# The stages of a transformer block in another sequence on every engine

## The chip, the cores and the metric

The kernel runs on one core of a Trainium2 chip. The metric is the device time of one execution in microseconds, the median over runs. PE is TensorE, DVE VectorE, ACT ScalarE, POOL GpSimd and SP SyncE, which issues most transfers.

## The reference

One layer over x of shape (2, 1024, 128): attention with 16 heads of 8 (layer norm of queries and keys per head, rotary turn, causal mask), then a mixture of 16 experts of 64, of which each token takes 2, and a shared one of 128.

```
x = x + attn(layernorm(x))
q, k = rope(headnorm(x @ Wq.T)), rope(headnorm(x @ Wk.T)); v = x @ Wv.T
out = softmax(mask(q k^T / sqrt(8))) v @ Wo.T + bo
x = x + ffn(layernorm(x))
s = softmax(x @ gate_w.T); groups of 4: keep 2 of 4 groups, then the 2 largest
y = sum_e combine[t, e] * ((silu(x We1 + be1) * (x We3 + be3)) We2 + be2)
z = silu(x ws1 + bs1) * (x ws3 + bs3) @ ws2 + bs2; return x + y + z
```

## The kernel before

The 2048 tokens are cut into four chunks of 512 (x = 0 to 3). Chunks 0 and 1 are the first halves of the two sequences, 2 and 3 the second halves. Heads go in four groups per chunk, so there are 16 attention blocks (a = 0 to 15). Each stage has a name with its indices, such as `scores.14.0`. All of them stand once in one long word list, `ORDER` (from line 132). Every engine walks the same list (`for kind, arg in SCHEDULE`) and issues the stages that are its own, so the list sets each engine's order, and semaphores set the rest. Behind an @ stand the PSUM banks that a PE stage fills; a fill waits until the reader of the bank's last fill is done (`wait_read`, line 592 on). Banks 0 to 5 are used in pairs by maxima and scores, bank 6 holds single fills and the sum of the experts, bank 7 the attention sum. Each engine executes its queue in order: a waiting stage holds what is behind it.

The stages by engine:
- PE: `xT`, `qkv` (line 635), `qT`, `kT` and other turns (626), `max` (644, 672: products whose maxima are wanted), `mturn` (681), `scores` (695, with the mask 644), `pv` (718), `proj` (728), `gate` (736), `moeU`, `moeV`, `moeG`, `moeL` (766), `moe_y` (782, 786), `wide` (758). Maxima and scores load 62 or 64 rows, two at a time in the array; `pv` loads 18 columns, four at a time; the products of 128 by 128 take the whole array.
- DVE: `norm`, `norm2` (1111 to 1127: for norm2.3 a chain of eleven small operations, each waiting for the one before), `headsum`, `maxred` (1159), `oturn`, `oT_read` (1174, 1176), `oback`, `proj_read`, `route1` to `route3` (1213 to 1242: the router's small chains), `moe_a` (1249), `moe_m` (1257), `moe_h_dve`, `final`.
- ACT: `exp` (842), the reads of `qkv` (858 to 862), `qT_lead`, `kT_lead`, `qT_mid`, `kT_mid` (bf16 parts of queries and keys), `norm_apply`, `norm2_apply` (923), `mcopy`, `moe_v`, `moe_t`, `moe_s`, and for chunk 0 the transfers of the keys' parts (`stack_act`).
- POOL: `norm_rstd`, `norm2_rstd` (1011 to 1020), `rstd_pool` (995 to 1002), `rope_pool` (472 to 478), `rope_join` (486, 487), `tables_pool` (449 to 454), `mneg` (1033, 1034: negated maxima split in two), `qT_low`, `kT_low` (1041), `moe_one` (1077), `moe_g` (1084), `moe_h` (496), `xbo`.
- SP: input transfers first, then `stack` (parts into q_st and k_st, line 507), `mrow` (567), `cstore`, `cload`, `store`.

The exponentials use eight slots, the values of the experts four (`V_RING`) and their products nine (`T_RING`), so `moe_v` waits for `moe_g` of three units earlier and `moe_t` for `moe_y` of nine earlier. A chunk's rotary chain is headsum, rstd_pool, rope_pool, rope_join, then qT and kT, the three parts and their transfers, then the maxima of the chunk.

Of the kernel before, what the change touches and what calls it, by code (L numbers as in the profile page):

```python
# [132 lines left out]
weights.0@5 ones.0 norm.0 weights_read.0 xT.0@6 xT_read.0 qkv.0@3 norm.1 norm_rstd.1 qkv_read.0 qkv.1@2 qkv_read.1  # L133
qkv.2@3 qkv.3@4 qkv_read.2 qkv_read.3 tables.0 norm_apply.1 xT.1@3 norm.2 xT_read.1 qkv.4@1 qkv.5@6 headsum.0 headrstd.0
rope.0 ones.1 qkv_read.4 qkv_read.5 qkv.6@5 qkv_read.6 qkv.7@0 qkv_read.7 qT.0@4 kT.0@3 norm_rstd.2 norm_apply.2
qT_lead.0 stack.0.0.0 kT_lead.0 qT_rest.0 qT_mid.0 xT.2@5 xT_read.2 kT_rest.0 kT_mid.0 halved.0 qkv.8@2 tables_pool.0
stack_act.0.1.0 headsum.1 qkv.9@4 qkv.10@0 qkv.11@6 qT_low.0 norm.3 stack_act.0.1.1 kT_low.0 stack_act.0.1.2 stack.0.0.2
qkv_read.8 qkv_read.9 qkv_read.10 qkv_read.11 stack.0.0.1 max.0.0@45 maxred.0.0 max.0.1@23 maxred.0.1 max.0.2@45
maxred.0.2 max.0.3@01 max.0.4@23 maxred.0.3 maxred.0.4 max.0.5@01 max.1.0@23 maxred.0.5 maxred.1.0 max.1.1@45 maxred.1.1
max.1.2@01 rstd_pool.1 rope_pool.1 maxred.1.2 max.1.3@23 maxred.1.3 max.1.4@45 maxred.1.4 mneg.0 mturn.0@0 mcopy.0  # L140
max.1.5@01 max.2.0@23 max.2.1@45 maxred.1.5 maxred.2.0 maxred.2.1 max.2.2@23 mrow.0 scores.0.0@01 exp.0.0 weights2.0@6
maxred.2.2 scores.0.1@45 max.2.3@01 maxred.2.3 max.2.4@23 maxred.2.4 weights2_read.0 exp.0.1 rope_join.1 qT.1@6 kT.1@5
scores.1.0@01 max.2.5@23 qT_lead.1 qT_rest.1 stack.1.0.0 kT_lead.1 exp.1.0 mneg.1 mturn.1@4 mcopy.1 qT_mid.1 kT_rest.1
mrow.1 pv.0 max.3.0@45 norm_rstd.3 norm_apply.3 maxred.2.5 mneg.2 maxred.3.0 kT_mid.1 scores.1.1@01 max.3.1@23
maxred.3.1 max.3.2@45 xT.3@6 exp.1.1 headsum.2 stack.1.1.0 scores.2.0@23 scores.3.0@01 maxred.3.2 qT_low.1 kT_low.1
stack.1.1.2 stack.1.0.1 xT_read.3 qkv.12@6 exp.2.0 exp.3.0 max.3.3@23 max.3.4@45 maxred.3.3 maxred.3.4 qkv.13@1 qkv.14@0
max.3.5@23 qkv_read.12 qkv_read.13 qkv_read.14 maxred.3.5 qkv.15@5 stack.1.1.1 stack.1.0.2 qkv_read.15 max.4.0@01
rstd_pool.2 mturn.2@6 mneg.3 max.4.1@23 scores.3.1@45 exp.3.1 rope_pool.2 maxred.4.0 max.4.2@01 pv.1 maxred.4.1
max.4.3@45 maxred.4.2 maxred.4.3 mcopy.2 scores.4.0@23 exp.4.0 max.4.4@01 pv.2 scores.4.1@45 maxred.4.4 max.4.5@23
mturn.3@6 maxred.4.5 mneg.4 scores.5.0@01 exp.4.1 exp.5.0 max.5.0@45 mrow.2 maxred.5.0 scores.6.0@23 mcopy.3 headsum.3  # L150
scores.6.1@01 max.5.1@45 pv.3 exp.6.0 mturn.4@6 exp.6.1 max.5.2@23 mcopy.4 rope_join.2 scores.7.0@01 exp.7.0 maxred.5.1
maxred.5.2 max.5.3@45 maxred.5.3 pv.4 pv.5 oturn.0 scores.7.1@23 max.5.4@45 maxred.5.4 scores.8.0@01 exp.7.1 xbo.0
qT.2@6 mrow.3 exp.8.0 scores.9.0@23 oT_read.0 max.5.5@45 maxred.5.5 qT_lead.2 qT_rest.2 scores.9.1@01 pv.6 exp.9.0
# [1240 lines left out]
```

## Time and profile before

| what | us |
|---|---|
| median of 3 runs | 383.33 |
| lowest and highest | 382.54, 387.38 |
| the profiled execution | 383.55 |
| its span, first to last instruction | 381.7 |
| granted clock of TensorE, mean | 0.95 |

The span leaves out what lies around the first and the last instruction, 1.85 us here. A matmul's duration in the rows holds its way through the array, so consecutive ones overlap, and the distance of their starts tells more than their length. A name such as `mx_diag` or `probs` is a tile; "<-" points from what is read to what is written. In the table by stage the five busy columns are PE, PEld (weight loads), DVE, ACT, POOL.

### The profile page before, as it was taken

The numbers are of one execution on the slowest core, as the hardware profiler recorded it, in microseconds if no ns is written. First come the engines' busy times: TensorE is split into PE (matmuls) and PEld (weight loads), VectorE is DVE, ScalarE is ACT, GpSimd is POOL, SyncE is SP. The second block draws the span as 40 slices with busy tenths as digits, with TensorE's granted clock in tenths as the row PEclk, the third lists the DMA queues.
The fourth block names the chain that finished last, engine by engine and source line by source line (L and its number), as shares of the span: only waits on it lengthen the run. The fifth ranks groups of instructions, "written<-read, shape, count | busy, mean of one in ns | idle before, by whom it ended". The sixth has DMA issues, their size and how long they took to land.

```text
span 381.7 us, 7937 instructions
## 1 busy us (share of the span) xinstructions
PE 338.2 (89%) x2883; PEld 148.3 (39%) x2883; DVE 291.7 (76%) x508; ACT 233.5 (61%) x340; POOL 181.1 (47%) x304
## 2 busy tenths in 40 slices
PE   2667689899799898999999989999999999969995
PEld 1233345445444334353334332434334433434342
DVE  5693789899999999779998899987686830656742
ACT  1656129776759566774576767786676999424320
POOL 1587985998855438657504502034060028471000
PEclk9966559999999999999999999999999999988999
DMA  4997004103200036002043130001000019000000
GB/s 124 200 217 162 16 3 127 43 3 92 78 3 4 0 106 149 2 0 72 0 100 87 38 75 2 3 1 30 2 2 2 3 53 202 0 0 0 3 27 27
DMA packets 26840, 19.65 MB, mean 51 GB/s; under 512 B 9713, under 2 KB 23570, under 8 KB 26738
## 3 DMA queue, kind: packets, MB, share of 16 engines
q1 hardware_dynamic: 25410, 18.09, 20.8%
q10 hardware_dynamic: 1392, 1.05, 1.2%
q8 instruction: 24, 0.39, 0.5%
q14 instruction: 14, 0.11, 0.1%
HBM read 11.56 MB, written 1.15 MB: 33 GB/s over the span
## 4 chain that ended last, share of the span: by engine, by line
PE 61%; DVE 24%; issue 5%; ACT 5%; DMA 2%; POOL 1%; ACTq 1%; SPq 1%; DVEq 0%; POOLq 0%
PE psum L766 14%; PE psum L718 13%; PE psum L782 7%; PE psum L695 7%; PE psum L672 7%; DVE mx_diag L1159 7%; PE psum L644 5%; DVE mx_full L1159 4%; ACT probs L842 2%; PE psum L626 2%; DVE mv L1249 2%; PE psum L635 1%; PE psum L736 1%; PE psum L728 1%; DVE resid L1148 1%
## 5 line engine op out<-in xcount | busy, mean ns | idle before, releaser
L842 ACT ACTIVATE probs<-psum 128x1024 f32<-128x1024 f32 x144 | 142.3, 1024 | 49.7 <-PE psum L644 27.1
L1159 DVE TENSOR_REDUCE mx_diag<-psum 128x4 f32<-128x512 f32 (+2 forms) x96 | 96.0, 1041 | 23.3 <-PE psum L672 22.6
L1159 DVE TENSOR_REDUCE mx_full<-psum 128x2 f32<-128x1024 f32 x64 | 76.1, 1220 | 7.3 <-PE psum L672 7.0
L718 PE MATMUL psum<-probs,v_ones 128*18 128x512 f32 (+3 forms) x768 | 73.6, 489 | 0.2
L766 PE MATMUL psum<-x2T,w 128*128 128x512 f32 x144 | 71.8, 626 | 1.0 <-DVE mv L1249 0.9
L672 PE MATMUL psum<-k_st,q_st 62*128 62x512 bf16 (+3 forms) x384 | 60.6, 344 | 2.0 <-ACT probs L842 0.9
L644 PE MATMUL psum<-masks 64*128 64x128 bf16 (+2 forms) x896 | 51.5, 216 | 11.0 <-DVE mx_diag L1159 3.3
L695 PE MATMUL psum<-q_st,k_st 64*128 64x512 bf16 (+3 forms) x384 | 53.7, 328 | 3.1 <-DVE mv L1249 0.9
L644 PEld LDWEIGHTS psum<-masks 64*128 64x128 bf16 x896 | 33.6, 96 | 42.8 <-DVE mx_diag L1159 14.9
L1077 POOL TENSOR_SCALAR mh<-mh 128x512 f32<-128x512 f32 x27 | 16.8, 623 | 62.3 <-ACT mh L895 62.1
L1084 POOL TENSOR_TENSOR mh<-mh,mv 128x512 f32<-128x512 f32 x27 | 34.1, 1270 | 11.8 <-DVE mv L1249 11.8
L766 PEld LDWEIGHTS psum<-x2T,w 128*128 128x128 f32 x144 | 25.7, 195 | 29.5 <-issue 24.4
L782 PE MATMUL psum<-mh,w 128*128 128x512 f32 x72 | 37.1, 624 | 0.0
L496 POOL TENSOR_TENSOR mh<-mh,early 128x512 f32<-128x512 f32 x24 | 30.6, 1287 | 12.6 <-DMA early<-combine_scratch 12.4
L695 PEld LDWEIGHTS psum<-q_st,k_st 64*128 64x128 bf16 x384 | 17.4, 94 | 41.8 <-ACT probs L842 18.1
L672 PEld LDWEIGHTS psum<-k_st,q_st 62*128 62x128 bf16 x384 | 20.2, 100 | 22.3 <-ACT probs L842 9.7
L1249 DVE SCALAR_TENSOR_TENSOR mv<-psum,b,mv 128x512 f32<-128x512 f32 x27 | 19.6, 743 | 9.7 <-ACT mh L895 9.3
L718 PEld LDWEIGHTS psum<-probs,v_ones 128*18 128x18 f32 x768 | 16.7, 97 | 25.3 <-issue 22.8
L886 ACT ACTIVATE mv<-psum,b3h 128x512 f32<-128x512 f32 x27 | 18.4, 687 | 11.0 <-PE psum L766 10.6
L1033 POOL CAST negmax<-mx_diag 128x16 bf16<-128x16 f32 x16 | 3.2, 198 | 43.3 <-DVE mx_diag L1324 40.2
L895 ACT ACTIVATE mh<-psum,b1h 128x512 f32<-128x512 f32 x27 | 18.5, 688 | 6.5 <-PE psum L766 6.4
L635 PE MATMUL psum<-w_qkv,xnT 128*128 128x384 f32 x32 | 19.0, 750 | 2.8 <-ACT xnT L848 2.7
(162 smaller groups left out, 359.0 us busy)
## 6 DMA issues: line engine op xcount, KB each, us to landing
early<-combine_scratch SPq DMA_DIRECT2D x24, 256.0 KB, 4.8
q_st<-parts SPq DMA_DIRECT2D x24, 128.0 KB, 2.4
k_st<-parts SPq DMA_DIRECT2D x18, 128.0 KB, 2.4
w<-in_We SPq DMA_DIRECT2D x3, 512.0 KB
k_st<-in_c_pad SPq DMA_DIRECT2D x8, 128.0 KB, 6.3
out<-xs SPq DMA_DIRECT2D x4, 256.0 KB, 2.3
xs<-in_x SPq DMA_DIRECT2D x3, 256.0 KB, 5.9
k_st<-parts ACTq DMA_DIRECT2D x6, 128.0 KB, 4.0
```

The source lines that it names most:

```text
L496: engine.tensor_tensor(h, h, comb_b[:, u, :], ALU.mult).then_inc(weighted, 1)
L635: pe.matmul(w[:, 0:3 * P], xnT[:, t * P:(t + 1) * P], w_qkv[:, :], start=True, stop=True).then_inc(work_full, 1)
L644: return pe.matmul(dst, masks[r, slot, :], blocked, start=start, stop=stop, skip_group_check=True)
L672: last = pe.matmul(w[:, par, i * keys:(i + 1) * keys], q_st[r, x % 2, 2 * g + m, q0:q0 + P], k_st[r, b, 2 * g + m, k0:k0 + keys], start=(w ...
L695: last = pe.matmul(w[:, par, col:col + cols], k_st[rows(par), b, 2 * g + m, kt * P:(kt + 1) * P], q_st[rows(par), x % 2, 2 * g + m, q0:q0 ...
L718: last = pe.matmul(acc[32 * j:32 * j + 2 * VC, q0:q0 + cols], own_then_zeros, probs[:, n % P_RING, j % 2, col:col + cols], start=(kt == 0 ...
L766: pe.matmul(w, (w1 if kind in ("moeU", "moeG") else w3)[:, unit(n), :], x2T[:, x % 2, :], start=True, stop=True).then_inc(work_full, 1)
L782: last = pe.matmul(y, w2[:, unit(n), :], mh[:, at % T_RING, :], start=(n == 0), stop=(n == UNITS - 1), skip_group_check=True)
L842: act.activation(probs[:, n % P_RING, :, :], wpair("scores", (s, i)), ACT.Exp, scale=SCALE).then_inc(exp_done, 1)
L1084: pool.tensor_tensor(t, t, mv[:, at % V_RING, :], ALU.mult).then_inc(gate_done, 1)
L1159: dve.tensor_reduce(dst[:, a % 2, :, pairs[0]:pairs[0] + nm, qt], w, AX.X, ALU.max, negate=True).then_inc(max_free, 1)
L1249: dve.scalar_tensor_tensor(out=v, in0=wbank("moeU", (x, n)), scalar=b1[:, unit(n):unit(n) + 1], in1=v, op0=ALU.add, op1=ALU.mult).then_inc ...
```

## The change

Only `ORDER` changes: the same 1316 words, each once, in another sequence, and other banks behind many PE stages. No function changes. Since every engine walks the list, this alters the order on PE, DVE, ACT, POOL and SP at once. The diff, cut to the stretches that the next sections speak of:

```diff
--- before.py
+++ after.py
@@ -130,127 +130,126 @@
 
 
 ORDER = """
-weights.0@5 ones.0 norm.0 weights_read.0 xT.0@6 xT_read.0 qkv.0@3 norm.1 norm_rstd.1 qkv_read.0 qkv.1@2 qkv_read.1
-qkv.2@3 qkv.3@4 qkv_read.2 qkv_read.3 tables.0 norm_apply.1 xT.1@3 norm.2 xT_read.1 qkv.4@1 qkv.5@6 headsum.0 headrstd.0
-rope.0 ones.1 qkv_read.4 qkv_read.5 qkv.6@5 qkv_read.6 qkv.7@0 qkv_read.7 qT.0@4 kT.0@3 norm_rstd.2 norm_apply.2
-qT_lead.0 stack.0.0.0 kT_lead.0 qT_rest.0 qT_mid.0 xT.2@5 xT_read.2 kT_rest.0 kT_mid.0 halved.0 qkv.8@2 tables_pool.0
-stack_act.0.1.0 headsum.1 qkv.9@4 qkv.10@0 qkv.11@6 qT_low.0 norm.3 stack_act.0.1.1 kT_low.0 stack_act.0.1.2 stack.0.0.2
-qkv_read.8 qkv_read.9 qkv_read.10 qkv_read.11 stack.0.0.1 max.0.0@45 maxred.0.0 max.0.1@23 maxred.0.1 max.0.2@45
-maxred.0.2 max.0.3@01 max.0.4@23 maxred.0.3 maxred.0.4 max.0.5@01 max.1.0@23 maxred.0.5 maxred.1.0 max.1.1@45 maxred.1.1
-max.1.2@01 rstd_pool.1 rope_pool.1 maxred.1.2 max.1.3@23 maxred.1.3 max.1.4@45 maxred.1.4 mneg.0 mturn.0@0 mcopy.0
-max.1.5@01 max.2.0@23 max.2.1@45 maxred.1.5 maxred.2.0 maxred.2.1 max.2.2@23 mrow.0 scores.0.0@01 exp.0.0 weights2.0@6
-maxred.2.2 scores.0.1@45 max.2.3@01 maxred.2.3 max.2.4@23 maxred.2.4 weights2_read.0 exp.0.1 rope_join.1 qT.1@6 kT.1@5
...
-mrow.1 pv.0 max.3.0@45 norm_rstd.3 norm_apply.3 maxred.2.5 mneg.2 maxred.3.0 kT_mid.1 scores.1.1@01 max.3.1@23
...
-exp.9.1 max.6.0@45 max.6.1@23 maxred.6.0 scores.10.0@01 kT.2@6 exp.10.0 maxred.6.1 mrow.4 scores.10.1@45 max.6.2@23
-maxred.6.2 max.6.3@01 kT_lead.2 exp.10.1 pv.7 rstd_pool.3 max.6.4@45 scores.11.0@23 exp.11.0 maxred.6.3 maxred.6.4
-max.6.5@01 stack.2.1.0 maxred.6.5 stack.2.0.0 pv.8 mneg.5 pv.9 max.7.0@45 qT_mid.2 kT_rest.2 kT_mid.2 stack.2.1.1
-max.7.1@23 scores.12.0@01 exp.12.0 pv.10 pv.11 maxred.7.0 maxred.7.1 mturn.5@4 mcopy.5 oturn.1 oT_read.1 oback.0
-scores.12.1@01 exp.12.1 scores.13.0@45 exp.13.0 max.7.2@23 maxred.7.2 rope_pool.3 scores.13.1@01 proj.0@6 proj_read.0
-norm2.0 exp.13.1 scores.14.0@23 exp.14.0 mrow.5 scores.15.0@01 max.7.3@45 pv.12 scores.15.1@23 exp.15.0 exp.15.1
-maxred.7.3 stack.2.0.1 max.7.4@01 qT_low.2 kT_low.2 mneg.6 mturn.6@6 max.7.5@45 scores.16.0@23 maxred.7.4 exp.16.0
-stack.2.0.2 stack.2.1.2 max.8.0@01 mcopy.6 maxred.7.5 maxred.8.0 norm2_rstd.0 norm2_apply.0 max.8.1@23 max.8.2@45 mneg.7
-maxred.8.1 pv.13 pv.14 pv.15 mturn.7@1 maxred.8.2 max.8.3@23 x2T.0@6 maxred.8.3 max.8.4@45 mcopy.7 x2T_read.0 maxred.8.4
-scores.16.1@01 max.8.5@23 exp.16.1 maxred.8.5 gate.0@6 gate_read.0 max.8.6@01 moeV.0.0@5 moeV.0.1@3 moe_v.0.0 maxred.8.6
...
-exp.73.1 scores.74.0@45 pv.70 route1.2 route2.2 exp.74.0 route3.2 cT.2@0 pv.71 cT_read.2 moe_t.2.2 moe_one.2.2
-scores.74.1@23 moe_a.2.2 moe_g.2.2 exp.74.1 moeV.2.4@4 moeU.2.3@0 cstore.2 moe_t.2.3 moe_one.2.3 moe_v.2.4 moe_a.2.3
-moe_g.2.3 moeV.2.5@1 moe_v.2.5 moeU.2.4@6 moe_t.2.4 scores.75.0@45 moe_one.2.4 scores.75.1@23 scores.76.0@01 moe_a.2.4
-store.1 cload.2.0 moe_h.2.1 pv.72 pv.73 pv.74 exp.75.0 exp.75.1 exp.76.0 scores.76.1@45 exp.76.1 scores.77.0@23 pv.75
-scores.77.1@45 moe_g.2.4 scores.78.0@01 exp.77.0 exp.77.1 moeU.2.5@6 exp.78.0 scores.78.1@45 scores.79.0@23 exp.78.1
-exp.79.0 pv.76 pv.77 pv.78 pv.79 cload.2.2 oturn.7 moeV.2.6@3 cload.2.1 moeV.2.7@1 moeV.2.8@4 moe_t.2.5 moe_a.2.5
-moe_h.2.2 moe_v.2.6 moe_v.2.7 moeU.2.6@2 moeU.2.7@0 moeU.2.8@1 oT_read.7 oback.3 proj.3@5 moe_v.2.8 moe_t.2.6 moe_t.2.7
-moe_h.2.3 moe_h.2.4 moe_one.2.5 moe_one.2.6 moe_a.2.6 moe_y.2.0 moe_one.2.7 moe_t.2.8 moe_one.2.8 cload.2.3 moe_y.2.1
-moe_y.2.2 moe_y.2.3 proj_read.3 norm2.3 norm2_apply.3 x2T.3@5 x2T_read.3 moe_g.2.5 moe_g.2.6 moe_h.2.5 moe_a.2.7
-moe_y.2.4 moe_g.2.7 moe_a.2.8 moe_g.2.8 gate.3@3 gate_read.3 moeG.3.0@5 moeG.3.1@0 moe_h.2.6 gate_exp.3 moe_s.3.0
-moe_s.3.1 route1.3 route2.3 moeG.3.2@3 moeG.3.3@1 moeL.3.0@5 moeL.3.1@4 moe_m.3.0 moe_m.3.1 moeL.3.2@2 moe_s.3.2
-moe_h.2.7 moe_s.3.3 moe_y.2.5 moe_h.2.8 route3.3 moe_y.2.6 moe_y.2.7 moe_y.2.8 y_leave.2 moeG.3.4@1 moe_s.3.4 moeG.3.5@4
-moe_s.3.5 moe_m.3.2 moeL.3.3@5 comb3.3 cT3.3@2 moe_m.3.3 moeL.3.4@6 moeL.3.5@0 cT3_read.3 wide.3.1@1 moe_m.3.4 moe_m.3.5
-moe_h_dve.3.1 wide.3.2@4 moe_h_dve.3.2 wide.3.3@2 wide.3.4@6 wide.3.5@3 moeG.3.6@5 moe_h_dve.3.3 moe_h_dve.3.4
-moeG.3.7@1 moe_h_dve.3.5 moe_s.3.6 moe_s.3.7 moeL.3.6@4 moe_m.3.6 moeL.3.7@0 yturn.2@3 moe_y.3.0 final.2 store.2 cT.3@4
-wide.3.6@1 moe_m.3.7 wide.3.7@5 wide.3.8@2 cT_read.3 moe_y.3.1 moe_y.3.2 moeG.3.8@0 moe_h_dve.3.6 moe_h_dve.3.7
-moe_y.3.3 moeL.3.8@4 moe_s.3.8 moe_m.3.8 moe_y.3.4 moe_y.3.5 moe_h_dve.3.8 moe_y.3.6 moe_y.3.7 moe_y.3.8 y_leave.3
-yturn.3@2 final.3 store.3
+ones.0 ones.1 weights.0@5 weights_read.0 norm.0 tables.0 xT.0@3 xT_read.0 qkv.0@1 qkv.1@0 norm.1 qkv_read.0 qkv_read.1
+qkv.2@6 qkv_read.2 qkv.3@1 qkv_read.3 norm_rstd.1 norm_apply.1 xT.1@5 xT_read.1 qkv.4@0 qkv.5@6 qkv_read.4 qkv_read.5
+qkv.6@2 qkv_read.6 qkv.7@5 norm.2 qkv_read.7 headsum.0 headrstd.0 rope.0 qT.0@1 qT_lead.0 stack.0.0.0 norm_rstd.2 kT.0@0
+kT_lead.0 headsum.1 qT_rest.0 kT_rest.0 stack_act.0.1.0 qT_mid.0 kT_mid.0 qT_low.0 stack_act.0.1.1 norm_apply.2 kT_low.0
+xT.2@2 stack_act.0.1.2 weights2.0@4 xT_read.2 weights2_read.0 stack.0.0.1 stack.0.0.2 max.0.0@45 max.0.1@23 maxred.0.0
+maxred.0.1 max.0.2@01 maxred.0.2 max.0.3@45 maxred.0.3 qkv.8@6 max.0.4@01 qkv_read.8 maxred.0.4 max.0.5@45 maxred.0.5
+max.1.0@23 maxred.1.0 max.1.1@01 qkv.9@6 rstd_pool.1 rope_pool.1 maxred.1.1 max.1.2@23 max.1.3@01 maxred.1.2 maxred.1.3
+mneg.0 max.1.4@45 qkv.10@2 qkv_read.9 qkv_read.10 maxred.1.4 rope_join.1 max.1.5@01 mturn.0@5 maxred.1.5 max.2.0@23
+maxred.2.0 max.2.1@01 mcopy.0 maxred.2.1 qkv.11@4 qkv_read.11 max.2.2@23 maxred.2.2 qT.1@4 norm.3 qT_lead.1 qT_rest.1
+kT.1@0 kT_lead.1 kT_rest.1 mrow.0 scores.0.0@23 exp.0.0 max.2.3@45 maxred.2.3 mneg.1 mturn.1@6 scores.0.1@23 norm_rstd.3
+qT_mid.1 max.2.4@01 stack.1.0.0 max.2.5@45 exp.0.1 maxred.2.4 scores.1.0@23 scores.1.1@01 kT_mid.1 mcopy.1 mrow.1
+stack.1.1.0 exp.1.0 pv.0 maxred.2.5 scores.2.0@23 exp.1.1 exp.2.0 norm_apply.3 headsum.2 max.3.0@01 max.3.1@45 qT_low.1
...
+max.4.2@45 maxred.4.0 maxred.4.1 max.4.3@01 mrow.2 maxred.4.2 qkv.13@6 qkv_read.13 max.4.4@23 max.4.5@45 rstd_pool.2
+mneg.3 pv.3 maxred.4.3 pv.4 mturn.3@6 tables_pool.0 mcopy.3 maxred.4.4 maxred.4.5 max.5.0@23 rope_pool.2 maxred.5.0
+scores.5.0@01 max.5.1@45 maxred.5.1 scores.6.0@23 mrow.3 exp.5.0 exp.6.0 pv.5 halved.0 oturn.0 mneg.4 scores.6.1@45
...
+exp.9.1 mneg.5 scores.10.0@45 scores.10.1@01 max.6.2@23 maxred.6.2 exp.10.0 exp.10.1 rstd_pool.3 qT.2@6 qT_lead.2
+max.6.3@45 max.6.4@23 maxred.6.3 scores.11.0@01 exp.11.0 pv.8 pv.9 xbo.0 mturn.5@5 qT_rest.2 mcopy.5 mrow.4 max.6.5@01
+maxred.6.4 maxred.6.5 max.7.0@45 maxred.7.0 kT.2@6 mrow.5 kT_lead.2 stack.2.1.0 kT_rest.2 scores.12.0@23 exp.12.0
+max.7.1@01 stack.2.0.0 maxred.7.1 scores.12.1@45 exp.12.1 pv.10 pv.11 scores.13.0@45 qT_mid.2 kT_mid.2 oturn.1
+scores.13.1@23 pv.12 exp.13.0 oT_read.1 oback.0 max.7.2@01 maxred.7.2 stack.2.0.1 scores.14.0@45 exp.13.1 exp.14.0
+mneg.6 proj.0@6 scores.15.0@23 exp.15.0 qT_low.2 proj_read.0 kT_low.2 norm2.0 scores.15.1@45 exp.15.1 pv.13 max.7.3@23
+maxred.7.3 scores.16.0@01 norm2_rstd.0 exp.16.0 max.7.4@45 mturn.6@2 mcopy.6 max.7.5@01 maxred.7.4 maxred.7.5
+rope_pool.3 stack.2.1.1 scores.16.1@23 exp.16.1 stack.2.1.2 stack.2.0.2 max.8.0@45 pv.14 maxred.8.0 pv.15 mneg.7
+max.8.1@23 max.8.2@01 norm2_apply.0 scores.17.0@45 exp.17.0 maxred.8.1 maxred.8.2 pv.16 max.8.3@23 mrow.6 x2T.0@6
+x2T_read.0 max.8.4@01 maxred.8.3 scores.18.0@45 maxred.8.4 max.8.5@23 maxred.8.5 gate.0@6 gate_read.0 moeV.0.0@1
+exp.18.0 gate_exp.0 moe_v.0.0 max.8.6@45 maxred.8.6 scores.18.1@23 exp.18.1 route1.0 moeV.0.1@6 moe_v.0.1 mturn.7@0
+mcopy.7 moeU.0.0@1 route2.0 max.8.7@45 max.8.8@23 moeV.0.2@0 moe_v.0.2 moe_t.0.0 moeU.0.1@6 moe_t.0.1 maxred.8.7
+maxred.8.8 rope_join.3 moe_a.0.0 moe_a.0.1 moeV.0.3@0 pv.17 moe_v.0.3 max.8.9@45 scores.19.0@01 exp.19.0 scores.19.1@23
+maxred.8.9 moeU.0.2@6 exp.19.1 scores.20.0@45 mrow.7 scores.21.0@01 max.8.10@23 exp.20.0 oturn.2 pv.18 scores.21.1@45
+exp.21.0 exp.21.1 route3.0 maxred.8.10 moe_one.0.0 moe_t.0.2 moe_g.0.0 pv.19 moe_one.0.1 pv.20 cT.0@5 cT_read.0
+max.8.11@01 scores.22.0@23 exp.22.0 maxred.8.11 max.8.12@45 max.8.13@01 maxred.8.12 maxred.8.13 mmin.8 mneg.8 xbo.1
+moe_a.0.2 qT.3@2 qT_lead.3 qT_rest.3 moeU.0.3@3 moe_t.0.3 moe_a.0.3 kT.3@4 moeU.0.4@5 kT_lead.3 moe_t.0.4 kT_rest.3
...
+exp.74.1 scores.75.0@23 exp.75.0 pv.72 pv.73 scores.75.1@45 scores.76.0@01 yturn.1@2 exp.75.1 exp.76.0 oT_read.6 final.1
+moeV.2.6@6 scores.76.1@45 exp.76.1 cload.2.3 moe_g.2.3 scores.77.0@23 exp.77.0 scores.77.1@01 pv.74 pv.75 exp.77.1
+cload.2.0 moe_h.2.1 moe_h.2.2 scores.78.0@45 exp.78.0 scores.78.1@23 scores.79.0@01 pv.76 pv.77 exp.78.1 pv.78 exp.79.0
+pv.79 moe_v.2.6 oturn.7 moeV.2.7@1 cload.2.1 moeU.2.5@2 moeU.2.6@5 moe_t.2.5 moe_t.2.6 moe_g.2.4 moe_h.2.3 moe_y.2.0
+moeV.2.8@3 moe_v.2.7 moe_v.2.8 oT_read.7 moe_h.2.4 cload.2.2 oback.3 proj.3@4 moeU.2.7@1 moe_a.2.5 moe_t.2.7 moe_a.2.6
+moeU.2.8@2 moe_one.2.5 moe_g.2.5 moe_one.2.6 moe_t.2.8 moe_y.2.1 moe_y.2.2 proj_read.3 norm2.3 norm2_apply.3 x2T.3@4
+moe_one.2.7 moe_a.2.7 x2T_read.3 moe_y.2.3 moeG.3.0@3 moe_a.2.8 moe_g.2.6 moe_h.2.5 moe_h.2.6 moe_g.2.7 moeG.3.1@1
+gate.3@5 moe_h.2.7 gate_read.3 gate_exp.3 route1.3 moe_s.3.0 moe_y.2.4 moe_y.2.5 moe_y.2.6 moeL.3.0@0 moeL.3.1@2
+moeG.3.2@3 moe_y.2.7 moe_s.3.1 moe_m.3.0 moe_m.3.1 moe_one.2.8 moeG.3.3@0 moe_g.2.8 moe_h.2.8 route2.3 route3.3 comb3.3
+moeL.3.2@4 moe_s.3.2 moe_s.3.3 moeL.3.3@5 moeL.3.4@0 moe_m.3.2 moe_m.3.3 moeL.3.5@1 store.1 moe_y.2.8 y_leave.2
+moeG.3.4@2 moeG.3.5@3 moeG.3.6@5 moe_s.3.4 moe_s.3.5 moe_s.3.6 cT3.3@2 cT3_read.3 moeG.3.7@4 moe_s.3.7 moe_m.3.4
+moe_m.3.5 moeL.3.6@3 moe_m.3.6 wide.3.1@0 wide.3.2@1 moe_h_dve.3.1 wide.3.3@5 wide.3.4@2 moe_h_dve.3.2 cT.3@4
+moe_h_dve.3.3 cT_read.3 moe_h_dve.3.4 moe_y.3.0 moe_y.3.1 moeG.3.8@3 yturn.2@1 moe_s.3.8 final.2 wide.3.5@2 wide.3.6@4
+wide.3.7@0 wide.3.8@3 moe_h_dve.3.5 moe_y.3.2 moe_h_dve.3.6 moeL.3.7@5 moeL.3.8@1 moe_y.3.3 moe_m.3.7 moe_h_dve.3.7
+moe_m.3.8 moe_y.3.4 moe_y.3.5 moe_y.3.6 moe_y.3.7 moe_h_dve.3.8 moe_y.3.8 y_leave.3 yturn.3@5 final.3 store.2 store.3
 """
 TOLD = [told(word) for word in ORDER.split()]
 SCHEDULE = [stage for stage, _ in TOLD]

```

## Rows read from the trace of the kernel before

**Rows 1.** The page: busy us, share of the span, instructions of each engine.

```profile
PE 338.2 (89%) x2883; PEld 148.3 (39%) x2883; DVE 291.7 (76%) x508; ACT 233.5 (61%) x340; POOL 181.1 (47%) x304
```

**Rows 2.** Table by stage: stretch, length, engine busy (instructions), clock, DMA share, GB/s.

```profile
40.00:57.00 17.00, 13.64 (x130) 7.26 (x131) 14.83 (x16) 2.47 (x4) 15.21 (x26) 0.50 0.01 1
...
40.80:104.70 63.90, 55.17 (x759) 29.48 (x755) 58.27 (x70) 38.69 (x61) 54.10 (x96) 0.87 0.19 52
...
104.00:325.00 221.00, 211.97 (x1934) 85.34 (x1935) 180.10 (x273) 158.35 (x202) 90.48 (x134) 1.00 0.17 40
...
325.00:382.00 57.00, 49.33 (x140) 21.80 (x132) 30.39 (x82) 16.41 (x26) 12.10 (x12) 0.93 0.03 10
```

**Rows 3.** Waits: who waited for whom, us in total, times, longest.

```profile
ACT probs L842 <- PE psum L644: 27.1, 28, 4.5
```

**Rows 4.** Order of time, 25 to 41 us: start, us, engine, line, operation.

```profile
25.75 0.32 POOL L449 TENSOR_TENSOR g_cos<-rope,gb 128x64 f32<-128x64 f32 x1
...
30.05 0.46 POOL L454 TENSOR_TENSOR g_add<-g_add,mh 128x128 f32<-128x128 f32 x1
...
30.65 4.50 SPq L507 DMA_DIRECT2D q_st<-parts  x6
...
32.64 3.46 ACTq L507 DMA_DIRECT2D k_st<-parts  x5
...
33.22 0.86 DVE L1111 BATCH_NORM_STATS2 stats<-xs 128x6 f32<-128x128 f32 x4
34.11 0.38 DVE L1114 BATCH_NORM_AGGREGATE mean_var<-stats 128x2 f32<-128x6 f32 x4
...
40.05 0.50 PE L644 MATMUL psum<-masks 64*128 64x256 bf16 x4 [2.75 <-ACT v_ones L862]
```

**Rows 5.** Order of time, PE at 172 us: three whole-array pairs, then a 64-row pair.

```profile
172.12 1.12 PE L782 MATMUL psum<-mh,w 128*128 128x512 f32 x2
173.09 1.02 PE L766 MATMUL psum<-x2T,w 128*128 128x512 f32 x2
173.94 1.02 PE L782 MATMUL psum<-mh,w 128*128 128x512 f32 x2
174.90 0.39 PE L672 MATMUL psum<-k_st,q_st 62*128 62x512 bf16 x2
```

**Rows 6.** Order of time, POOL, 91 to 111 us: rope_pool.3, norm2_rstd.0, mneg.7, rope_join.3.

```profile
91.59 2.37 POOL L472 TENSOR_TENSOR early<-early,hrstd 128x1024 f32<-128x1024 f32 x1
...
101.47 0.20 POOL L1011 TENSOR_SCALAR nr_pool<-mean_var 128x4 f32<-128x4 f32 x1 [0.44 <-DVE mean_var L1114]
...
106.39 0.22 POOL L1034 TENSOR_TENSOR negmax<-mx_diag,negmax 128x16 bf16<-128x16 f32 x1
...
108.61 2.35 POOL L487 TENSOR_TENSOR roped<-roped,early 128x1024 f32<-128x1024 f32 x1
```

**Rows 7.** Order of time: line 1233 beside a POOL product, and with POOL idle.

```profile
120.54 1.23 DVE L1233 TENSOR_TENSOR beats<-beats 128x64 f32<-128x64 f32 x1
...
120.40 1.28 POOL L1084 TENSOR_TENSOR mh<-mh,mv 128x512 f32<-128x512 f32 x1
...
346.62 0.22 DVE L1233 TENSOR_TENSOR beats<-beats 128x64 f32<-128x64 f32 x1
```

**Rows 8.** Order of time: the chain of norm2.3 on DVE, and POOL beside it.

```profile
334.68 1.19 DVE L1099 TENSOR_SCALAR seed<-rstd 128x4 int32<-128x4 int32 x1
335.91 0.16 DVE L1101 SCALAR_TENSOR_TENSOR nr<-seed 128x4 f32<-128x4 f32 x1
...
334.58 1.26 POOL L496 TENSOR_TENSOR mh<-mh,early 128x512 f32<-128x512 f32 x1
```

**Rows 9.** Order of time, PE, 325 to 340 us: the tail's start.

```profile
325.32 5.42 PE L766 MATMUL psum<-x2T,w 128*128 128x512 f32 x12
330.58 1.05 PE L728 MATMUL psum<-w_o,o_normT 128*128 128x128 f32 x8
...
339.57 0.66 PE L626 MATMUL psum<-ident,w_raw 128*128 128x128 f32 x4 [3.26 <-ACT w_raw L923]
```

More of the change, by code:

```diff
@@ L148 @@
[L148 to L152, printed above, removed]
@@ new lines @@
+moe_h.0.1 moe_h.0.2 moe_a.0.6 qT_mid.3 proj_read.1 norm2.1 moeU.0.7@0 exp.26.0 moe_one.0.5 moeU.0.8@6 scores.26.1@23
+moe_t.0.7 moe_a.0.7 cload.0.2 moe_one.0.6 exp.26.1 max.9.8@45 maxred.9.8 pv.24 norm2_rstd.1 scores.27.0@23 max.9.9@01
+moe_t.0.8 scores.27.1@45 pv.25 exp.27.0 scores.28.0@23 exp.27.1 maxred.9.9 moe_a.0.8 exp.28.0 max.9.10@01 max.9.11@45
+maxred.9.10 moe_y.0.0 maxred.9.11 max.9.12@01 maxred.9.12 max.9.13@23 maxred.9.13 max.10.0@45 moe_y.0.1 norm2_apply.1
+kT_mid.3 x2T.1@2 x2T_read.1 moe_y.0.2 maxred.10.0 scores.28.1@01 exp.28.1 max.10.1@23 maxred.10.1 scores.29.0@45
@@ new lines @@
+moe_g.0.5 exp.29.0 moe_g.0.6 moe_h.0.3 moe_h.0.4 moe_y.0.3 moe_one.0.7 moe_one.0.8 max.10.2@01 max.10.3@23 maxred.10.2
+maxred.10.3 moe_g.0.7 moe_g.0.8 moe_h.0.5 moe_h.0.6 max.10.4@45 moe_y.0.4 maxred.10.4 moeV.1.0@0 moe_v.1.0 gate.1@1
+moeV.1.1@2 gate_read.1 moeV.1.2@0 gate_exp.1 route1.1 moe_v.1.1 moe_v.1.2 max.10.5@45 mmin.9 mneg.9 scores.29.1@23
+maxred.10.5 exp.29.1 moeU.1.0@1 moeU.1.1@0 moe_t.1.0 moe_a.1.0 moe_t.1.1 moe_a.1.1 moeU.1.2@3 moe_t.1.2 moe_a.1.2
+moeV.1.3@2 moe_v.1.3 moe_y.0.5 max.10.6@45 maxred.10.6 max.10.7@23 maxred.10.7 mturn.9@1 mcopy.9 moeU.1.3@0 moe_t.1.3
@@ new lines @@
+scores.56.1@23 exp.56.1 cload.1.3 maxred.14.3 max.14.4@01 maxred.14.4 pv.54 max.14.5@45 max.14.6@23 mneg.13 mturn.13@1
+mcopy.13 pv.55 max.14.7@01 maxred.14.5 maxred.14.6 scores.57.0@45 exp.57.0 moeU.1.8@6 max.14.8@23 max.14.9@45
+maxred.14.7 norm2_rstd.2 maxred.14.8 norm2_apply.2 scores.57.1@01 moe_h.1.2 moe_g.1.6 mrow.13 exp.57.1 max.14.10@23
+maxred.14.9 moe_t.1.8 moe_g.1.7 maxred.14.10 moe_a.1.8 pv.56 scores.58.0@45 exp.58.0 scores.59.0@01 exp.59.0 yturn.0@2
+final.0 x2T.2@6 x2T_read.2 max.14.11@45 max.14.12@23 maxred.14.11 maxred.14.12 scores.59.1@01 exp.59.1 pv.57 pv.58
@@ new lines @@
+scores.68.0@45 scores.68.1@23 oturn.6 exp.67.1 exp.68.0 exp.68.1 moe_g.1.8 moe_y.1.6 moe_y.1.7 moe_g.2.0 moe_h.1.8
+moe_y.1.8 y_leave.1 moe_g.2.1 scores.69.0@23 scores.69.1@45 scores.70.0@01 pv.66 pv.67 exp.69.0 exp.69.1 exp.70.0
+scores.70.1@23 exp.70.1 pv.68 mmin.15 mneg.15 mturn.15@5 mcopy.15 scores.71.0@01 scores.71.1@23 scores.72.0@45 exp.71.0
+exp.71.1 exp.72.0 route1.2 route2.2 route3.2 moeV.2.3@6 moe_v.2.3 moeU.2.3@1 moeV.2.4@3 moeV.2.5@0 moeU.2.4@6 moe_t.2.3
+mrow.15 moe_g.2.2 moe_v.2.4 moe_v.2.5 cT.2@2 cT_read.2 cstore.2 pv.69 moe_a.2.3 scores.73.0@23 scores.73.1@01
```

130 lines of the change are left out of this document (53 added, 77 removed).

## The prediction

> **What bounds the kernel now.** I read the page's busy times first: TensorE (PE) is busy for 338.2 of 381.7 us, VectorE (DVE) for 291.7, ScalarE for 233.5, GpSimd (POOL) for 181.1 [rows 1]. The table by stage [rows 2] says where this matters. From 104 to 325 us PE is busy 212.0 of 221.0 us and DVE 180.1: there PE sets the pace and idle DVE time is free. From 40.8 to 104.7 us DVE is busy 58.3 of 63.9 and POOL 54.1, PE 55.2: three engines are nearly full. From 40 to 57 us the granted clock is 0.50, so PE is at 1.2 GHz. The first 40 us wait for input: the first maxima start at 40.05 us, right after the last of the 12 transfers of split queries and keys that were issued from 30.65 us on [rows 4]. The tail after 325 us is one dependent chain with PE work laid into its gaps. The waits [rows 3] show that the longest wait of ScalarE, 27.1 us, ends on PE's products, which agrees with PE as the pace.
>
> **The change part by part.** Every stage is in both lists, once, so instruction counts and sizes are equal and only positions and PSUM banks differ. I sum for each engine, from the durations in the trace, what stands ahead of a stage in the old and in the new list; a PE stage counts with its start-to-start time where nothing waits (whole-array product 0.85 to 0.86 us, qkv 0.65 at full clock, pv 0.86 for two banks, maxima and scores 0.22 to 0.39).
>
> *PE's tile shapes.* With three shapes (64 rows for maxima and scores, 18 columns for probabilities times values, the whole array for the rest; the small turns counted with their column width) the old list changes shape 236 times, the new one 244 times, so the runs don't get longer as a whole. The price: a whole-array pair starts 0.85 us before the next one of its shape, and 0.96 us before a 64-row one [rows 5], 0.11 us. 8 x 0.11 = +0.9 us. By stretch the counts are 46 and 54 between max.0.0 and max.8.0, 181 and 181 from there to the last pv, 8 and 8 in the tail: all eight more lie in the first, and its sum below holds them. The Trainium skill, TensorEngine Tiling (Array Packing), section Key Properties, says that changing the tiling mode drains the engine. By that rule the new list would pay for more drains and not fewer; the trace agrees on the sign, and its 0.11 us is used.
>
> *Up to 40 us.* The four qkv products of chunk 2, norm.3, halved and tables_pool leave the shadow of the input transfers; ScalarE issues the transfers of the leading keys before its two middle parts and before norm_apply.2. The first of these can't leave before 28.9 us, and 12 transfers of 128 KB share the queues, so max.0.0 starts at about 39.7 us instead of 40.05: -0.3 us, between -0.8 and +0.5. weights2 now stands ahead of it and asks for 11 input transfers, which were issued before the ones that the maxima wait for, so it costs nothing.
>
> *40 to 104 us.* DVE takes norm.3 (0.86 + 0.38 us [rows 4]) and halved (0.3) here, +1.6 us; it has 5.6 us idle in this stretch [rows 2], so between 0 and 1.6 of it shows, and I take 1.0 because the idle pieces are short and the maxima queue behind each reduction. PE takes the four qkv products (2.6 us), and pv.13 (0.9) and scores.16.1 (0.4) come ahead of max.8.0, weights2 (0.3) leaves, and there are the eight changes of shape: +4.5 us at full clock from max.0.0 to max.8.0, of which 1.3 are taken from the next stretch. It has 8.7 us idle here and pays half clock for the first 17 us, where four products are 5.1 us against 2.6 us. Covered if DVE stays the slower one; if not, up to +2.5. POOL takes tables_pool, from 25.75 to 30.5 us before [rows 4], 4.8 us, between mneg.3 and rope_pool.2: it was free and now stands in a full stretch. rope_join.2 ends 4.8 us later, at about 87.5 us; behind it on POOL wait mneg.5, rstd_pool.3, mneg.6 and the low parts of chunk 2. The reader of rope_join.2 is the turn qT.2, which has 44.2 us of PE work ahead of it instead of 38.7, 5.5 us more, so the delay is covered by 0.7 us.
>
> *The second POOL shift.* rope_pool.3 (6.7 us) stood before norm2_rstd.0 and fills 91.6 to 98.2 us; now it follows it. norm2_rstd.0 waits for DVE's statistics at 101.5 us in either order [rows 6], a little over 1 us later now, so POOL idles before it, ends it at 107.4, rope_pool.3 at 114.1, mneg.7 at 114.6 (106.6 before), rope_join.3 at 119.0 (111.0 before). mneg.7 releases mturn.7, which has 67.0 us of PE work ahead of it, 58.8 before; PE reached that sum at 116.2 us. Slack 1.6 us, cost 0. x2T.0 needs norm2_apply.0 at 109.2 us and PE reaches it near 110.6.
>
> *104 to 325 us.* PE's sum from max.8.0 to pv.79 is 1.4 us smaller: pv.13, scores.16.1 and moeU.2.5 are gone from it, moeV.2.6 came in, and nothing changes in the count of shapes: -1.4 us. On DVE, short operations that read two SBUF operands last until a running POOL instruction ends: 1.23 us against 0.22 free, beside a POOL product of 1.28 us [rows 7]. route2 and route3 of chunks 0 and 1 and two o_norm scalings lose 6.9 us in all to this. In the new list route2.1, route3.0, route3.1 and these scalings have POOL waiting or busy with little; route1.0 and route2.0 fall beside rope_join.3, whose two instructions can hold them for up to 3 us. Net DVE gain 3.9 us. As PE is 96% busy in this stretch I let a third pass, -1.2 us; bounds 0 and -3.9.
>
> *The tail.* Between the last pv and proj.3 stand six products, 325.32 to 330.58 us [rows 9]; now five, and proj.3's input is ready at 328.3 us in either order: -0.9 us. Against it stands norm2.3, the chain of eleven tiny operations on which all that follows waits. Two of them were held by POOL (1.19 us for one of 0.16 [rows 8]), then POOL ran out of work. In the new order moe_one.2.7, moe_g.2.6, moe_h.2.5 and moe_h.2.6 lie beside the chain, so three or four are held: +1.2 us, between 0 and +3.6. From x2T.3 to the last product PE's sum grows by 0.8 us: +0.8. The half-clock stretch there begins after PE idles 3.3 us before x2T.3 [rows 9]; the gap stays, so I keep its cost. Tail: -0.9 + 1.2 + 0.8 = +1.1 us.
>
> The Trainium skill, SBUF — State Buffer, section Who interferes with whom, says that a VectorE instruction with two SBUF inputs contends with a GpSimd instruction that reads SBUF and that the loser blocks fully. If every one of the eleven operations met a fresh POOL instruction this would be some 11 us instead of 4; POOL runs out of ready work after four.
>
> Sum: -0.3 + 1.0 + 0 - 1.4 - 1.2 + 1.1 = -0.8 us. The profiled execution took 383.55 us (span 381.7), the median of the runs is 383.33. 383.3 - 0.8 = 382.5 us.
>
> **The rivals.**
> A, the sum holds, the order is worth about nothing (0.58): 382.5 us, own range 378 to 387.
> B, POOL becomes the bound (0.20). For it: 54.1 of 63.9 us busy before, plus 4.8, plus the idle before norm2_rstd.0. Slacks of 0.7 and 1.6 us are thin. Against it: PE work was laid in front of both readers. If mneg.7 comes 9.4 us late instead of 8 and the queries of chunk 2 miss their place, maxima of chunk 2 (max.8.0) start late and each turn waits; it decides from a slip of some 3 us, and gives 383.3 + 4.8 to + 9.4, so about 390.
> C, DVE is the hidden pace (0.20). For it: in 40.8 to 104.7 us DVE is fullest. If all contention goes (6.9 us), and PE's idle 9.0 us from 104 to 325 halves, it gives 383.3 - 1.4 - 6.9 = 375 us. Against it: PE is 96% busy when the contention occurs.
> D, norm2.3 is held at nearly every step (0.02 alone, part of the upper range): 11 x 1.1 = 12 us minus the 2.1 already paid, 392 us. Against: POOL's four instructions are 4.4 us long.
>
> **How the numbers follow.** A is likeliest, so 382.5 us. The range reaches into B and C: 376 to 391. Over 2% faster means under 375.7, slower means over 391.0, about what a measurement of this kernel can tell from no change. C lies on the first limit and gives 0.16 with a little of A; B and D give 0.19; within 2% is 0.65.
>
> **What would show it.** max.0.0 at 39 to 40.5 us. max.8.0 at 104.5 to 106 us, with POOL busy through 57 to 99 us. mneg.7 near 114.6 us and no wait of mturn.7 for it over 1 us; a wait there is B. Routing stages of chunk 1 free of held operations, and route1.0 or route2.0 held. The last pv at 323 to 326 us: earlier than 320 is C. norm2.3 taking 5.5 to 8 us, and proj.3 4.3 us after the last pv. I am wrong if PE's small waits, 8.7 us idle from 40.8 to 104.7 and 9.0 from 104 to 325 [rows 2], change by more than 4 us, because no row prices them one by one.

## The result, and the profile after

The new kernel takes 389.81 us in the median, the kernel before 383.28 us beside it: ratio 1.0191, 95% interval 1.0161 to 1.022, so 6 to 8 us slower. The first profiled execution of the new kernel was a disturbed one of 1067 us; all rows of the new kernel below are from a second profiled execution of the same kernel, which took 391.47 us (span 389.6).

The page of the new kernel, busy times (they answer to [rows 1]) and the granted clock in 40 slices:

```profile
PE 337.5 (87%) x2883; PEld 145.8 (37%) x2883; DVE 294.9 (76%) x508; ACT 234.5 (60%) x340; POOL 178.0 (46%) x304
...
PEclk9965899999998999999899998999999999978999
```

The same row of the kernel before:

```profile
PEclk9966559999999999999999999999999999988999
```

The busy times hardly moved, but the row of the clock has single digits of 8 in the middle, where the kernel before has 9 throughout. The table by stage (columns as in [rows 2]) and three short stretches around those digits:

```profile
40.00:57.00 17.00, 12.44 (x122) 6.42 (x117) 16.76 (x26) 6.47 (x17) 14.09 (x20) 0.93 0.02 5
40.80:104.70 63.90, 54.98 (x779) 28.92 (x775) 59.13 (x80) 43.48 (x73) 50.96 (x101) 0.99 0.19 52
104.00:325.00 221.00, 208.50 (x1806) 81.43 (x1803) 181.17 (x273) 151.29 (x193) 89.95 (x133) 0.98 0.14 33
...
124.00:128.00 4.00, 4.00 (x32) 1.59 (x34) 3.66 (x13) 2.95 (x4) 0.97 (x2) 0.57 0.01 2
185.00:189.00 4.00, 4.00 (x40) 1.38 (x40) 3.47 (x7) 0.71 (x1) 0.00 (x0) 0.59 0.02 6
233.00:237.00 4.00, 4.00 (x26) 0.87 (x24) 3.29 (x4) 1.84 (x3) 0.25 (x2) 0.57 0.00 0
```

Three times between 104 and 325 us TensorE falls to its lower level (1.2 GHz) for most of 4 us; in [rows 2] it ran at 1.00 in this whole stretch. And PE idles 221.0 - 208.5 = 12.5 us there against 9.0 before; time at half clock counts as busy in this column. The first 17 us of maxima run nearly at full clock now (0.93 against 0.50), which brings little, because DVE is busy for 16.76 of 17.

Where the time went, from the starts of the same stages in both traces (us from start to start):

| stretch | before | new | difference |
|---|---|---|---|
| start to max.0.0 | 40.05 | 39.04 | -1.0 |
| max.0.0 to max.8.0 | 63.74 | 65.86 | +2.1 |
| max.8.0 to pv.79, the last pv | 220.99 | 227.07 | +6.1 |
| pv.79 to proj.3 | 5.80 | 4.94 | -0.9 |
| proj.3 to x2T.3 | 9.00 | 10.34 | +1.3 |
| x2T.3 to final.3 | 38.73 | 38.95 | +0.2 |

The sum is +7.9 us, and the stretch that was to get 2.6 us shorter got 6.1 us longer. PE waits in three places there. The first, in order of time (columns as in [rows 7]):

```profile
115.39 2.39 DVE L1215 TENSOR_TENSOR lg<-lg,gate_bb 128x64 f32<-128x64 f32 x1
...
115.35 2.35 POOL L486 TENSOR_TENSOR roped<-roped,early 128x1024 f32<-128x1024 f32 x1
...
121.85 0.34 PE L643 MATMUL psum<-masks 64*128 64x256 bf16 x4 [1.78 <-DVE mx_full L1158]
```

One of route1.0's small operations is held for the whole of rope_join.3's second product; route1.0 takes 3.96 us (1.68 free). Behind it on DVE stand route2.0 and the two reductions for whose banks PE waits 1.8 us. The second place:

```profile
178.91 1.30 POOL L1051 TENSOR_TENSOR xs<-xs,bo_b 128x512 f32<-128x512 f32 x1
179.01 1.29 DVE L1230 TENSOR_TENSOR beats<-gsm 128x64 f32<-128x64 f32 x1
...
180.18 2.49 POOL L495 TENSOR_TENSOR mh<-mh,early 128x512 f32<-128x512 f32 x2
180.34 1.20 DVE L1231 TENSOR_TENSOR beats<-beats,lower 128x64 f32<-128x64 f32 x1
...
181.56 1.19 DVE L1232 TENSOR_TENSOR beats<-beats 128x64 f32<-128x64 f32 x1
...
182.79 0.22 DVE L1233 TENSOR_REDUCE gsm<-beats 128x16 f32<-128x64 f32 x1
...
184.84 0.34 PE L643 MATMUL psum<-masks 64*128 64x256 bf16 x4 [2.83 <-DVE mv L1248]
```

POOL has work back to back (xbo.2, moe_h.0.7, moe_h.0.8), and each small operation of route2.1 lasts until one of these ends: 5.03 us for the stage, 1.60 free. moe_a.1.4, whose bank max.10.9 needs, stands behind it. The third place is on the transfers:

```profile
221.86 3.91 SPq L581 DMA_DIRECT2D early<-combine_scratch  x6
226.34 1.41 SPq L566 DMA_DIRECT2D q_st<-maxT  x2
...
231.68 0.39 PE L694 MATMUL psum<-q_st,k_st 64*128 64x512 bf16 x2 [1.51 <-DMA q_st<-maxT]
```

mturn.11 stands 11 us later than before, only 5.9 us ahead of scores.45.0, and SP issues its two small transfers (mrow.11) right behind six of 256 KB with the weights of the experts. After each of the three waits comes one of the three stretches of half clock.

### The profile page after: what moved, and what is told of

The parts are those of the page before. It is cut to its first block, busy times and chain, and to the rows that moved or that the text cites. A ratio compares the mean times of both kernels' runs of the same rounds, so it can differ in the third digit from the quotient of the medians.

```text
span 1065.1 us, 7936 instructions
## 1 busy us (share of the span) xinstructions
PE 1042.4 (98%) x2883; PEld 305.0 (29%) x2883; DVE 295.1 (28%) x508; ACT 241.6 (23%) x340; POOL 175.5 (16%) x304
## 3 DMA queue, kind: packets, MB, share of 16 engines
HBM read 11.56 MB, written 1.15 MB: 12 GB/s over the span
## 4 chain that ended last, share of the span: by engine, by line
PE 97%; ACT 1%; DVE 1%; DMA 0%; ACTq 0%; issue 0%
PE psum L765 23%; PE psum L717 22%; PE psum L781 11%; PE psum L694 11%; PE psum L671 11%; PE psum L643 7%; PE psum L634 4%; PE psum L625 3%; PE psum L785 1%; PE psum L727 1%; PE psum L735 1%; PE psum L743 1%; PE psum L757 1%; DMA xs<-in_x 0%; ACTq L506 0%; ACT early L922 0%
## 5 line engine op out<-in xcount | busy, mean ns | idle before, releaser
L765 PE MATMUL psum<-x2T,w 128*128 128x512 f32 x144 | 246.3, 1926 | 0.0
L717 PE MATMUL psum<-probs,v_ones 128*18 128x512 f32 (+3 forms) x768 | 240.9, 1415 | 0.0
L671 PE MATMUL psum<-k_st,q_st 62*128 62x512 bf16 (+3 forms) x384 | 152.2, 843 | 0.0
L694 PE MATMUL psum<-q_st,k_st 64*128 64x512 bf16 (+3 forms) x384 | 143.5, 833 | 0.2 <-ACT probs L841 0.2
L781 PE MATMUL psum<-mh,w 128*128 128x512 f32 x72 | 124.3, 1915 | 0.0
L643 PE MATMUL psum<-masks 64*128 64x128 bf16 (+2 forms) x896 | 116.5, 418 | 0.7 <-ACT w_o L847 0.4
L643 PEld LDWEIGHTS psum<-masks 64*128 64x128 bf16 x896 | 75.8, 185 | 120.2 <-issue 115.7
L765 PEld LDWEIGHTS psum<-x2T,w 128*128 128x128 f32 x144 | 59.4, 432 | 120.8 <-issue 113.4
L781 PEld LDWEIGHTS psum<-mh,w 128*128 128x128 f32 x72 | 29.4, 428 | 62.4 <-issue 60.6
L634 PE MATMUL psum<-w_qkv,xnT 128*128 128x384 f32 x32 | 41.0, 1443 | 1.5 <-ACT xnT L847 1.5
```

The source lines that it names most:

```text
L634: pe.matmul(w[:, 0:3 * P], xnT[:, t * P:(t + 1) * P], w_qkv[:, :], start=True, stop=True).then_inc(work_full, 1)
L643: return pe.matmul(dst, masks[r, slot, :], blocked, start=start, stop=stop, skip_group_check=True)
L671: last = pe.matmul(w[:, par, i * keys:(i + 1) * keys], q_st[r, x % 2, 2 * g + m, q0:q0 + P], k_st[r, b, 2 * g + m, k0:k0 + keys], start=(w ...
L694: last = pe.matmul(w[:, par, col:col + cols], k_st[rows(par), b, 2 * g + m, kt * P:(kt + 1) * P], q_st[rows(par), x % 2, 2 * g + m, q0:q0 ...
L717: last = pe.matmul(acc[32 * j:32 * j + 2 * VC, q0:q0 + cols], own_then_zeros, probs[:, n % P_RING, j % 2, col:col + cols], start=(kt == 0 ...
L765: pe.matmul(w, (w1 if kind in ("moeU", "moeG") else w3)[:, unit(n), :], x2T[:, x % 2, :], start=True, stop=True).then_inc(work_full, 1)
```

## The experiments

All edits are moves of words in `ORDER`; a word marked - goes, one marked + comes. The new kernel again, unaltered (391.26 us median of two runs, 391.05 and 391.47):

> The changed kernel unaltered, for a profile that can be read against the one before. If POOL became the bound (rival B): mneg.7 near 116 us or later and max.8.0 at 107 us or later, with most of the 6.5 us lost by 110 us. If the loss is in the tail (the chain norm2.3 held by POOL at more steps than four): the last pv before 326 us and norm2.3 longer than 8 us. If it is PE's small waits in between: PE's idle from 104 us to the last pv grows by 4 us or more.

One edit in the new kernel for each of the three places, and all three together (e4):

```diff
 exp.18.1
-route1.0
...
-route2.0
...
 maxred.8.8
+route1.0
+route2.0
```

(e1),

```diff
 scores.29.1@23
+route2.1
 maxred.10.5
...
 cload.0.3
-route2.1
```

(e2), and, as e3,

```diff
 mmin.11
+mneg.11
...
 max.12.3@01
+mturn.11@6
+mcopy.11
+mrow.11
 moeV.1.6@6
...
-mneg.11
...
-mturn.11@5
-mcopy.11
...
-mrow.11
 scores.45.0@01
```

> The new kernel with one edit: route1.0 and route2.0 stand behind maxred.8.7 and maxred.8.8 on DVE instead of ahead of them, so they no longer run inside rope_join.3 while two reductions that PE needs are queued behind them. Held-chain theory (H): the 1.9 us wait of PE before max.8.9 at 121.8 us and the dip of the granted clock at 124.0 to 127.4 us go; worth 1.9 + 1.7 = 3.6 us at most, and I expect 1.5 to 3 us less than the new kernel, about 388 us. Rival (S, the loss is spread over many small waits and does not hang on this place): within 0.7 us of the new kernel, since the wait comes back a few stages later.

Measured: 388.98 us, ratio to the kernel before 1.0179 (1.0099 to 1.0258), 0.8 us less than the new kernel where 1.5 to 3 were expected. There is no dip at 124 us, but the wait moved: 2.2 us before scores.19.0, for moe_a.0.0, which now stands behind both router stages and ends at 122.71 us, 0.15 us ahead of scores.19.0. That the dip is gone can't be laid to the edit: e2 and e3 below leave this place alone and have none there either.

> The new kernel with one edit: route2.1 moves up on DVE from behind moe_a.1.3 (178.9 us, amid six POOL stages back to back) to between mmin.9 and maxred.10.5 (171.4 us, where POOL idles). H: route2.1 takes 1.6 to 2.3 us instead of 5.03, the 2.8 us wait of PE before max.10.9 at 184.8 us and the dip of the granted clock at 185.5 to 188.9 us go; 2.5 to 4.5 us less than the new kernel, about 387 us. S: within 0.7 us of the new kernel.

Measured: 387.0 us, 1.0133 (1.0067 to 1.0199). route2.1 takes 1.59 us, the wait and the dip at 185 us are gone, and the stretch from max.9.0 to max.11.0 fell from 59.1 to 56.1 us. This one is firm: the five profiles with route2.1 in its old place (new, e1, e3, e9, e11) have 58.1 to 60.7 us there, the six with it early (e2, e4, e5, e6, e7, e10) 55.8 to 56.1.

> The new kernel with one edit: mneg.11, mturn.11, mcopy.11 and mrow.11 move up, from 225.8 us to about 216.5 us on PE, ahead of the combine weights' transfers cload.1.x on SP, to bank 6. H: the row of maxima arrives long before scores.45.0, the 1.5 us wait of PE at 231.7 us and the dip of the granted clock at 233.3 to 236.7 us go; 1.5 to 3 us less than the new kernel, about 388.5 us. S: within 0.7 us of the new kernel.

Measured: 387.5 us, 1.0157 (1.0055 to 1.0259). No wait before scores.45.0 and no dip; from max.11.0 to max.15.0 77.2 us instead of 79.4.

> The new kernel with the three edits of the three single runs together. H: the sum of the three, 6 to 9 us less than the new kernel, so 381 to 384 us, equal to the kernel before; no half-clock dip between 110 and 340 us, and the last pv starts at about 325 us. S: less than 2.5 us gained, 387 us or more.

Measured: 384.8 us, 1.0063 (1.0018 to 1.0109), so 5 us less than the new kernel, where 6 to 9 were expected. There is no half clock between 110 and 340 us, and the last pv starts at 325.66 us. The three places are most of the loss. The single runs are not told apart from the new kernel by their times (the intervals overlap), only by their traces; this one is.

Then the router of chunk 0 in other places, and the two theories of the third place. Against e4:

```diff
 maxred.8.8
-route1.0
-route2.0
...
 moe_a.0.1
+route1.0
...
 maxred.8.9
+route2.0
```

(e5, which keeps the edits of e2 and e3), and, as e6, the same without the edit of e3 but with

```diff
 cstore.1
-cload.1.2
-cload.1.1
...
-cload.1.0
...
 mrow.11
+cload.1.2
+cload.1.1
+cload.1.0
 scores.45.0@01
```

> The new kernel with route2.1 and mturn.11 moved as in the run of all three, but with the router of chunk 0 in other places: moe_a.0.0 and moe_a.0.1 first, then route1.0, then maxred.8.9, then route2.0. In the run of all three the wait of PE at 121 us did not go, it moved: 2.2 us before scores.19.0, until moe_a.0.1 had read its bank, which stood behind both router stages. H: with nothing that PE waits for behind two router stages this wait shrinks to under 1 us, and the kernel is 1 to 2.5 us shorter than with all three (384.8), so about 383 us. S: the wait comes back elsewhere, within 0.7 us of 384.8.

Measured: 385.23 us, 1.0063 (1.003 to 1.0096), against what the held-chain theory expected: the wait came back as 1.5 us before scores.20.0 and 1.1 us before pv.18. Both later places for the router only shifted it. (In e4 too the wait before scores.19.0 ends with moe_a.0.0 and not with moe_a.0.1.)

> As e5_routes_apart, but mturn.11 stays late (5.9 us ahead of scores.45.0) and instead the three transfers of combine weights cload.1.x stand behind mrow.11 on SP. Two theories of the 1.5 us wait for mrow.11. Q (the row queues behind 1.5 MB of combine weights that keep the DMA engines busy from 222 to 230 us): no wait before scores.45.0, time as e5_routes_apart, within 0.7 us. L (the turn is simply too late, the row takes its 4 to 5 us anyway): a wait of 1 to 1.6 us and perhaps a dip of the clock remain, 1 to 3 us more than e5_routes_apart.

Measured: 384.08 us, 1.0034 (0.9998 to 1.0071), 1.15 us less than e5 where no more than 0.7 either way was expected. Order of time, SP and PE:

```profile
222.20 1.37 SPq L566 DMA_DIRECT2D q_st<-maxT  x2
223.67 3.95 SPq L581 DMA_DIRECT2D early<-combine_scratch  x6
...
225.96 0.39 PE L694 MATMUL psum<-q_st,k_st 64*128 64x512 bf16 x2
```

The turn is as late in the list as in the new kernel, but scores.45.0 starts 3.8 us after the issue of mrow.11, without a wait (no bracket), where it started 5.3 us after it. So it was what stood ahead of it in the queue, not the late turn. The Trainium skill, DMA: Bandwidth & Descriptors, section Issuing engines are not separate DMA queues, says that all transfers share the same 16 DMA engines; these rows agree, as two transfers of 4 KB took 5.3 us behind 1.5 MB and at most 3.8 us ahead of it.

Is it the place of the router stages or their being held? This edit touches POOL alone:

```diff
 maxred.8.8
-rope_join.3
...
 moe_one.0.0
+rope_join.3
```

> The new kernel with one edit on POOL alone: rope_join.3 stands behind moe_one.0.0 and so starts at about 119.6 us instead of 113.3 us; DVE's order isn't touched, route1.0 and route2.0 still stand ahead of maxred.8.7. It tells whether the stages hurt because POOL holds them or because of their place. H (held): route1.0 takes 1.7 us instead of 3.96 and route2.0 1.6 instead of 1.90, the wait of PE before max.8.9 falls from 1.9 us to under 0.6 us, the dip of the granted clock at 124 us goes; 1.5 to 3.5 us less than the new kernel (389.8), about 387.5 us. P (place): the two router stages ahead of the reductions cost as much when free, wait of 1.5 us or more, within 0.7 us of the new kernel. Against both: route3.0 at 125 us could now be held by what rope_join.3 pushes back, which would give back up to 1 us.

Measured: 388.95 us, 1.0156 (1.0074 to 1.0239), 0.9 us less than the new kernel where 1.5 to 3.5 were expected. Order of time, POOL, DVE and PE:

```profile
120.92 1.97 POOL L485 TENSOR_TENSOR early<-early,g_add 128x1024 f32<-128x1024 f32 x1
...
116.61 0.22 DVE L1215 TENSOR_TENSOR lg<-lg,gate_bb 128x64 f32<-128x64 f32 x1
...
125.44 1.20 DVE L1188 TENSOR_TENSOR lg<-lg,rank 128x64 f32<-128x64 f32 x1
...
129.43 0.60 PE L743 MATMUL psum<-ident,lg 128*16 128x128 f32 x4 [1.65 <-DVE lg L1241]
```

With DVE's order as it was, line 1215 takes 0.22 us instead of 2.39 and PE doesn't wait before max.8.9. From the start of route1.0 to the end of the reduction behind route2.0 DVE takes 4.57 us instead of 7.16: they were held, it was not their place. (PE also came later, max.8.0 starts at 106.24 us and not at 104.90, so not all of the missing wait is the edit's.) But what rope_join.3 pushes back on POOL now holds route3.0 (5.24 us, 3.27 in the new kernel), and cT.0 waits 1.65 us for it, more than the 1 us expected.

Last the tail, alone in the new kernel, on top of e5 (e7), in the kernel before (e8, with route2.0 behind route1.0), and, as e10, the edits of e9, of e2, of e6 on cload.1.x and this one together:

```diff
 moe_t.2.7
-moe_a.2.6
...
 norm2.3
+moe_a.2.6
 norm2_apply.3
```

> The new kernel with one edit: moe_a.2.6 behind norm2.3, so that three POOL stages leave the chain's side. H: norm2.3 3.7 us instead of 6.79 (3.1 us), the gap before x2T.3 falls from 4.9 to 1.8 us, and the half-clock stretch at 346 to 353 us does not come, which gives 1 to 3.4 us more: 4 to 6 us less than the new kernel (389.8), about 385 us. T: only the 3.1 us of the chain, about 386.7 us, the clock dips as before.

Measured: 386.19 us, 1.0126 (1.0089 to 1.0164), 3.6 us less than the new kernel where 4 to 6 were expected. norm2.3 takes 3.71 us, PE waits 1.53 us before x2T.3 instead of 4.60, and the half clock behind it doesn't come; from the last pv to the end the trace has 53.0 us instead of 57.7, 4.7 less. route1.3 is held in exchange (4.27 us instead of 1.69), as in e7 and e10.

> e5_routes_apart with one more edit: moe_a.2.6 stands behind norm2.3 on DVE, so moe_g.2.6, moe_h.2.5 and moe_h.2.6 on POOL can't start until the chain of eleven small operations is over. H: norm2.3 takes 3.7 to 4.5 us instead of 6.78 and x2T.3 starts that much earlier after proj.3; 2.0 to 3.0 us less than e5_routes_apart, about 380.5 us, less than the kernel before. Rival (T): the POOL work displaced returns as a wait of moe_y.2.5 and later ones for moe_h.2.5, and no more than 0.7 us is gained.

Measured: 381.03 us, 0.9979 (0.994 to 1.0019), 4.2 us less than e5, where 2 to 3 were expected: more than the three us of the chain, as the half clock goes too, as in e11.

> The kernel before with two edits: route2.0 directly behind route1.0 (POOL idles there from 111 to 117 us; it took 3.50 us at 119 us beside moe_one and moe_g, 1.60 free), and moe_a.2.6 behind norm2.3, so that moe_g.2.6 and moe_h.2.5 don't run beside it. H: route2.0 takes 1.6 us, norm2.3 takes 3.5 to 4.5 us instead of 5.44; the first is worth 0 to 1 us as PE waits little there, the second 1 to 2 us: 1 to 3 us less than the kernel before. T: within 0.7 us of it.

Measured: 380.07 us, 0.9954 (0.9917 to 0.9991). route2.0 takes 1.60 us and norm2.3 3.65; it is ahead of the kernel before by 2.2 us at the last pv and by 4.0 at x2T.3, though in the tail route1.3 is held now (4.84 us instead of 1.68). This trace is of the fastest of its ten runs (377.89 us); by the medians it is 3.05 us ahead.

> The new kernel with four edits: rope_join.3 behind moe_one.0.0, route2.1 early, cload.1.x behind mrow.11, moe_a.2.6 behind norm2.3. H: 378.5 to 380.5 us, less than e7_norm2_3_apart (381.0), because the wait of 1.6 + 1.2 us near 124 us is gone too, and below the kernel before (383.1). T: 381 us or more, that is the place at 120 us gives nothing.

Measured: 378.98 us, 0.9904 (0.9869 to 0.994). Its page's clock, the table of the stretch, norm2.3's operation that had been held, and x2T.3:

```profile
PEclk9975699999999999999999999999999999999999
...
104.00:325.00 221.00, 212.36 (x1927) 84.51 (x1927) 178.49 (x274) 158.50 (x201) 95.60 (x141) 1.00 0.17 40
...
332.89 0.17 DVE L1098 TENSOR_SCALAR seed<-rstd 128x4 int32<-128x4 int32 x1
...
336.76 0.66 PE L625 MATMUL psum<-ident,w_raw 128*128 128x128 f32 x4 [1.53 <-ACT w_raw L922]
```

So four moves of words turn an order that was 1.9% slower than the kernel before into one that is 1% faster. But two such moves in the kernel before (e8) already give 0.9954: e8 is 3.05 us ahead of the kernel before beside it, e10 3.47 us, and the intervals overlap. So the runs don't show that the new order, once mended, is better than the old one mended the same way; from max.8.0 to the last pv they take 218.65 (e8) and 218.35 us (e10).

**What is a wait and what is the clock?** The same code ran in several of these kernels with a wait and a dip, with the wait alone, and with neither (us from start to start; w a wait of PE of 1.1 us or more inside the stretch, d dip):

| stretch | new | e1 | e2 | e3 | e9 | e10 | e11 |
|---|---|---|---|---|---|---|---|
| max.8.0 to max.9.0 | 31.78 w d | 29.91 w | 29.37 d | 29.76 w | 29.40 w | 29.41 w | 33.47 w d |
| max.9.0 to max.11.0 | 59.11 w d | 60.72 w d | 56.08 | 59.22 w d | 58.08 w | 55.83 | 59.73 w d |
| max.11.0 to max.15.0 | 79.36 w d | 77.64 w | 79.46 w d | 77.22 | 79.56 w d | 76.30 | 77.50 w |
| max.15.0 to pv.79 | 56.81 | 56.82 | 56.82 | 56.82 | 56.81 | 56.81 | 56.81 |

At 184 us in e9 PE waits as long as in the new kernel, but its clock stays full; at 231 us it falls in e9, behind a wait of 1.70 us, and not in e1, behind one of 1.28 (the clock is the third number from the end; the last row is of e1):

```profile
184.03 0.34 PE L643 MATMUL psum<-masks 64*128 64x256 bf16 x4 [2.84 <-DVE mv L1248]
...
185.00:189.00 4.00, 3.95 (x48) 1.08 (x40) 3.76 (x11) 2.63 (x3) 0.00 (x0) 1.00 0.02 4
231.00:235.00 4.00, 4.00 (x26) 0.73 (x25) 2.78 (x3) 1.89 (x3) 0.00 (x0) 0.62 0.00 0
```

```profile
231.00:235.00 4.00, 3.63 (x30) 1.21 (x30) 2.66 (x3) 2.65 (x3) 0.00 (x0) 1.00 0.00 0
```

The wait of 2.8 us at 185 us costs 58.08 - 55.83 = 2.2 us alone, the dip 59.11 - 58.08 = 1.0 more. At 231 us the wait costs 77.64 - 76.30 = 1.3 us (e1 against e10). The new kernel takes 79.36 - 77.64 = 1.7 us more, 0.2 of it for its longer wait and 1.5 for the dip: behind the wait, from scores.45.0 to max.15.0, it takes 43.48 us against 41.98.

The first place is less settled. The order there is that of the new kernel in e2, e3 and e11 too (e2's dip comes from a wait of 1.67 us before max.8.0), and the stretch took 29.37, 29.76 and 33.47 us in them. It depends on when DVE arrives: in e2 it comes to line 1215 after rope_join.3 has ended, and nothing is held (start, us, and POOL beside it):

```profile
118.24 0.23 DVE L1215 TENSOR_TENSOR lg<-lg,gate_bb 128x64 f32<-128x64 f32 x1
...
115.77 2.35 POOL L486 TENSOR_TENSOR roped<-roped,early 128x1024 f32<-128x1024 f32 x1
```

Against e3 the dip is worth 1.5 us (14.83 us against 13.33 from max.8.9 to max.9.0) and the longer wait (1.78 us against 1.27) 0.5; against e10 0.4 us are left. Together some 4.7 us of waits and 4.0 of half clock make up the 227.07 - 218.35 = 8.7 us that lie between the new kernel's profile and that of e10 in this stretch. That profile is of a run 1.7 us above the median of the kernel.

## Why the prediction was wrong, point by point

*Up to 40 us: right in direction.* max.0.0 at 39.04 us, forecast 39.7 with bounds of 39.25 and 40.55, so a little earlier than allowed for; 38.8 to 39.9 over the profiles of new orders read here.

*40 to 104 us: right in place.* max.8.0 at 104.90 us, forecast 104.5 to 106. The stretch from max.0.0 grew by 2.1 us where the sum had 1.0; with the same words up to there it grew by 1.2 to 3.3 us in the other runs of new orders, so one profile doesn't size this term. The price of a change of shape, 0.11 us, isn't safe either: [rows 5] has 0.97 us between its first two pairs, which have the same shape. At most 0.9 us hung on it.

*The POOL shifts and rival B: right, and B fell.* These rows answer to [rows 6]:

```profile
101.67 0.20 POOL L1010 TENSOR_SCALAR nr_pool<-mean_var 128x4 f32<-128x4 f32 x1 [3.27 <-DVE mean_var L1113]
...
106.33 2.37 POOL L471 TENSOR_TENSOR early<-early,hrstd 128x1024 f32<-128x1024 f32 x1
...
113.14 0.22 POOL L1033 TENSOR_TENSOR negmax<-mx_diag,negmax 128x16 bf16<-128x16 f32 x1
```

mneg.7 is done at 113.4 us (forecast 114.6) and mturn.7 starts at 114.66 without a wait for it. tables_pool took 2.8 us there, not the 4.8 of [rows 4], and rope_join.2 ended at 84.9 us (forecast 87.5).

*104 to 325 us: wrong, and this decided it.* Three steps failed.

First, "In the new list route2.1, route3.0, route3.1 and these scalings have POOL waiting or busy with little". route2.1 had POOL busy back to back and took 5.03 us, longer than before (2.84), while route3.0 and route3.1 came free as forecast (3.27 and 3.30 us; 4.70 and 4.63 before). I had compared positions in the two lists and not the times at which POOL would work off what had piled up in its queue. Second, "As PE is 96% busy in this stretch I let a third pass". A share of busy time over 221 us doesn't price a hold that stands ahead of the reads PE needs next; the 3.4 us by which route2.1 was held cost 2.2 us, and the 2.0 us by which route1.0 was held in e3 cost 0.4. That route1.0 would be held beside rope_join.3 was foreseen, but priced by this third too. Third, mrow.11 and the weights' transfers on SP were not in the sum at all, though both moved: 1.3 to 1.5 us. Of the relief of 3.9 us on DVE nothing came: it is busy for 180.6 us between max.8.0 and pv.79, 180.3 before.

And the clock was carried over as 1.00 from [rows 2]. The kernel before kept it in this profile with no wait above 1 us there; the new order didn't: 4.0 us, nearly half of the 8.7, and none of it in the sum.

The forecast of this stretch came out where the holds are gone, though partly by luck. In e10 this stretch takes 218.35 us, 2.64 less than before, against -1.4 - 1.2 = -2.6 forecast, and DVE is busy 176.7 us between max.8.0 and pv.79 against 180.3 before: 3.6 us of relief, forecast 3.9. But e10 has edits that the prediction didn't have, and the old order with its own route2.0 freed (e8) takes 218.65 us: most of the 2.6 is had without the new order. How the 2.64 splits between PE's sum and the relief isn't shown, and no run here prices a change of tile shape by itself.

*The tail: right in the main.* +0.7 us from the last pv to the end, forecast +1.1. proj.3 4.94 us after the last pv (-0.9, as forecast); from x2T.3 on it took 0.2 us more, forecast 0.8. norm2.3, the answer to [rows 8], and x2T.3, to [rows 9]:

```profile
340.31 1.20 DVE L1098 TENSOR_SCALAR seed<-rstd 128x4 int32<-128x4 int32 x1
341.54 1.18 DVE L1100 SCALAR_TENSOR_TENSOR nr<-seed 128x4 f32<-128x4 f32 x1
342.76 1.19 DVE L1101 TENSOR_TENSOR nr<-nr,rstd 128x4 f32<-128x4 f32 x1
343.98 0.16 DVE L1102 SCALAR_TENSOR_TENSOR seed<-nr,seed 128x4 f32<-128x4 f32 x1
...
340.22 1.27 POOL L1083 TENSOR_TENSOR mh<-mh,mv 128x512 f32<-128x512 f32 x1
341.44 2.48 POOL L495 TENSOR_TENSOR mh<-mh,early 128x512 f32<-128x512 f32 x2
...
347.25 1.12 PE L625 MATMUL psum<-ident,w_raw 128*128 128x128 f32 x4 [4.60 <-ACT w_raw L922]
```

Three operations are held, 6.79 us instead of 5.44, +1.35 where +1.2 was forecast; rival D (held at every step) fell. That the gap before x2T.3 would stay at 3.3 us was wrong, it grew by the same 1.3 us. What was missed is how much the chain is worth when it is free: the gap before x2T.3 shrinks from 4.6 to 1.5 us and takes the half clock with it.

The condition named at the end, that PE's idle time would change by more than 4 us, was not met to the letter: 8.9 us from 40.8 to 104.7 (8.7 before), 12.5 from 104 to 325 (9.0 before), +3.5. It pointed at the right place, but counted idle time alone, and half clock passes for busy. Rival C (DVE as the hidden pace, faster) named the right resource, and e10 reached 3.6 of its 6.9 us of relief by other moves; the time it gave, 375 us, wasn't reached. The case that came, slower because held chains stand ahead of PE's reads, was not among the rivals; that 389.8 us still lies within 376 to 391 is luck: the range reached so far up for rival B, which didn't happen.

## What to carry to other kernels

Where two engines share a resource, a chain of short operations can be held again at each of its operations, each time for what is left of an instruction of the other engine. So look up at what time that engine will be working off a backlog, not what stands beside the chain in the list; and then which reads are queued behind it. A small transfer on the path goes ahead of the large ones in its queue, even if its data comes a little later. And an order that gives PE a wait of 1.5 to 3 us can pay for it once more in clock, 1.0 to 1.5 us here each time it fell. When the same code takes 29 to 33 us in different executions, one profile of an edit isn't enough to credit the edit.

## What the runs showed of the hardware

- A small DVE operation beside POOL work back to back takes what is left of one POOL instruction, each anew: 1.29, 1.20 and 1.19 us in route2.1, 0.22 free. TENSOR_REDUCE takes 0.22 us beside the POOL operation that follows these (182.79 us), and 0.21 us (line 1212, 114.55 us) beside rope_join.3's first product. One with a single SBUF input is held too: line 1098, TENSOR_SCALAR, 1.20 us against 0.17. The Trainium skill, SBUF — State Buffer, section Who interferes with whom, says that a tensor_scalar can enter a mode that takes the shared ports and that a reduction never does; both agree with these rows.
- Half clock in the middle of a kernel whose PE is 96% busy: every stretch of it between 104 and 325 us, in the thirteen profiles read here, lay at or right behind a wait of PE of 1.5 us or more (up to 2.9), and the two kernels without such a wait (before and e8) had none. But of 19 such waits 11 came with it and 8 without, and the same wait falls on either side: 2.83 us before max.10.9 with it in the new kernel, 2.84 without it in e9; 1.52 us before scores.20.0 with it in e5, without it in e6. Which of them falls isn't settled by these runs.
- The wait of 4.6 us before x2T.3 came with half clock in each of the eight profiles that have it, the one of 1.5 us in none of four.
